# First and last units of a fused attention and FFN kernel replanned: identity first, beta's product in fp32r parts, last FFN pair in two jobs

## The reference, cut to what matters

```python
# x: (2, 1024, 256), 16 heads of 128, FFN 256 -> 256 with ternary weights
def layer(x):
    n = layernorm(x)                                  # eps 1e-5, no gamma and beta
    q, k, v = (einsum('bsd,hed->bhse', n, W) for W in (W_Q, W_K, W_V))
    scores = where(causal, -1e9, einsum('bhse,bhme->bhsm', q, k) / sqrt(128))
    z = einsum('bhsm,bhme->bhse', softmax(scores), v)
    x = x + einsum('bhse,hde->bsd', z, W_O)
    m = layernorm(layernorm(x)) * gamma + beta        # the inner one without gamma, beta
    w = clip(round(W / (mean(abs(W)) + 1e-5)), -1, 1)
    return x + einsum('bsi,oi->bso', m, w) + bias
```

## Time and profile before

| | us |
|---|---|
| median of 3 runs | 816.5 |
| lowest and highest | 816.1, 816.52 |
| the profiled execution's own time | 813.95 |
| its span (first to last instruction) | 811.9 |
| PE busy | 801.7 (99%) |
| DVE busy | 666.5 (82%) |
| ACT busy | 557.1 (69%) |
| POOL busy | 547.4 (67%) |
| DMA queue of SP | 57.0% of the 16 engines' span |

### The profile page before, as it was taken

The page is one execution under the profiler, slowest core; times in us unless marked ns, Lnnn a source line. Parts: engine busy times, 40 slices in busy tenths (PEclk is TensorE's granted clock), DMA queues, the critical chain, the costliest instruction groups (busy, mean ns, idle before and its releaser), DMA issues.

```text
span 811.9 us, 14642 instructions
## 1 busy us (share of the span) xinstructions
PE 801.7 (99%) x4846; PEld 722.6 (89%) x4846; DVE 666.5 (82%) x1470; ACT 557.1 (69%) x1031; POOL 547.4 (67%) x280
## 2 busy tenths in 40 slices
PE   8999999999999999999999999999999999999998
PEld 7988998888999898899888899888889888899887
DVE  8988787888787878878878878788878788878988
ACT  6877667667666667666766766766766766766684
POOL 6188755696666856768557885568665686676486
PEclk9999999999999999999999999999999999999999
DMA  6366766456656565666655676546656655555603
GB/s 189 82 147 146 176 140 142 117 132 170 141 137 143 137 153 128 138 151 149 162 124 119 149 175 144 140 108 146 167 132 143 145 128 130 130 137 137 144 13 105
DMA packets 57226, 111.49 MB, mean 137 GB/s; under 512 B 16960, under 2 KB 21184, under 8 KB 57152
## 3 DMA queue, kind: packets, MB, share of 16 engines
q1 hardware_dynamic: 57152, 110.56, 57.0%
HBM read 10.88 MB, written 2.10 MB: 16 GB/s over the span
## 4 chain that ended last, share of the span: by engine, by line
PE 92%; DVE 3%; SPq 2%; DMA 1%; POOL 1%; issue 1%; ACT 0%; POOLq 0%; ACTq 0%
PE scores L701 23%; PE ring L654 23%; PE ring L634 21%; PE ring L643 11%; PE ring L664 10%; SPq L452 2%; PE ring L673 1%; DMA pT<-turn 1%; PE ring L598 1%; PE scores L763 1%; POOL norm L544 1%; DVE acc L878 1%; DVE stats L896 0%; PE scores L691 0%; DVE scores L858 0%
## 5 line engine op out<-in xcount | busy, mean ns | idle before, releaser
L528 POOL TENSOR_TENSOR pT<-pT 128x1024 fp32r<-128x1024 f32 x186 | 444.7, 2412 | 251.7 <-ACT pT L799 251.6
L792 ACT ACTIVATE turn<-scores,negmax 128x128 f32<-128x128 f32 (+7 forms) x256 | 189.0, 739 | 154.5 <-DVE negmax L858 88.3
L858 DVE CUSTOM_DVE_ANT_0 scores<-scores,mask 128x128 f32<-128x128 f32 (+7 forms) x256 | 192.7, 763 | 101.7 <-PE scores L701 100.5
L701 PE MATMUL scores<-kT,qT 128*128 128x512 f32 (+2 forms) x1056 | 224.9, 350 | 1.2 <-ACT turn L792 1.2
L654 PEld LDWEIGHTS ring<-pT,v 128*128 128x128 f32 x1116 | 188.0, 189 | 24.8
L654 PE MATMUL ring<-pT,v 128*128 128x512 f32 x1116 | 209.8, 342 | 0.0
L799 ACT ACTIVATE pT<-pT 128x1024 fp32r<-128x1024 f32 x186 | 196.4, 1057 | 16.3 <-DMA pT<-turn 15.4
L701 PEld LDWEIGHTS scores<-kT,qT 128*128 128x128 f32 x1056 | 175.5, 188 | 20.6 <-ACT turn L792 2.2
L866 DVE STREAM_TRANSPOSE turn<-turn 128x128 f32<-128x128 f32 (+1 forms) x248 | 187.1, 764 | 0.0
L664 PE MATMUL ring<-wo_s,zT 128*128 128x256 f32 x768 | 113.3, 284 | 0.2 <-DVE zT L929 0.2
L878 DVE SCALAR_TENSOR_TENSOR acc<-ring,inv,acc 128x256 f32<-128x256 f32 x256 | 109.5, 469 | 0.0
(11 more groups left out here) (84 smaller groups left out, 553.4 us busy)
## 6 DMA issues: line engine op xcount, KB each, us to landing
pT<-turn SPq DMA_DIRECT2D x496, 128.0 KB, 2.3
pT<-turn SPq DMA_DIRECT2D x496, 64.0 KB, 2.0
acc<-in_x SPq DMA_DIRECT2D x8, 256.0 KB, 5.3
wk_raw<-in_wk SPq DMA_DIRECT2D x8, 256.0 KB, 2.9
wq_raw<-in_wq SPq DMA_DIRECT2D x8, 256.0 KB, 3.8
wv_raw<-in_wv SPq DMA_DIRECT2D x8, 256.0 KB, 3.0
norm<-in_wo SPq DMA_DIRECT2D x8, 256.0 KB, 2.9
out<-acc SPq DMA_DIRECT2D x8, 256.0 KB, 2.2
```

The source lines that it names most:

```text
L528: pool.tensor_tensor(chunk(half, LO, c), f32(chunk(half, LO, c)), f32(chunk(half, HI, c)), ALU.subtract).then_inc(plo_ready, 1)
L701: mm = pe.matmul(scores[:, t % 2, first + c:first + c + n], qT[:, par, a, t * P:(t + 1) * P], kT[:, par, m, c:c + n], start=(i == 0), stop ...
L792: act.activation(turned, columns, ACT.Exp, bias=negmax[:, t % 2:t % 2 + 1], scale=-1.0, accum_out=rowsum[:, u % 2, t:t + 1]).then_inc(prob ...
L858: dve.tensor_tensor_reduce(out=tile, in0=tile, in1=mask[:, S - (t + 1) * P:S], scale=-1.0, scalar=FAR, op0=ALU.add, op1=ALU.min, accum_out ...
```

## The change

The lists of the steady units stay as they are. The START and END lists are written anew with the same jobs, with these differences of content:

- POOL makes the identity and its copy before anything else, under a semaphore of their own (`ident_ready`), and PE waits for that alone. The mask follows. The clear of `turn1` moves from before the three weight splits to behind them.
- 50 instead of 48 warm-up products ahead, 30 instead of 34 behind the first two transposes.
- ACT's second `std` stands before its half of `("x", 1)` instead of behind it.
- POOL splits beta into two fp32r parts (`("beta",)`), and makes the ternary weights before its first norm instead of behind its third. The product with beta is four fp32r matmuls instead of two fp32 ones, and stands much earlier in the list.
- The last FFN pair is two jobs, `("ff", 7, 0)` and `("ff", 7, 1)`, each with an addition and a store of its own.

`tiles_of` and the new branch in `wait_norm` make room for a norm shared by two engines; no item in the lists uses it.

```diff
-WARM_UP = 48
+WARM_UP = 50
 START_TENSOR = (
-    ("x", 0), ("x", 1), ("warm", 34), ("qk", 2, 0), ("x", 2), ("x", 3), ("qk", 0, 0), ("qk", 0, 1), ("qk", 3, 0),
+    ("x", 0), ("x", 1), ("warm", 30), ("qk", 2, 0), ("x", 2), ("qk", 0, 0), ("x", 3), ("qk", 0, 1), ("s", 0, 0),
...
 START_SCALAR = (
-    ("std", 0), ("std", 1), ("norm", 0), ("norm", 1), ("x", 0), ("x", 1), ("std", 2), ("norm", 2), ("norm", 3),
+    ("std", 0), ("std", 1), ("norm", 0), ("norm", 1), ("x", 0), ("std", 2), ("x", 1), ("norm", 2), ("norm", 3),
...
@@ def store
-                sp.wait_ge(job_taken, job["ff", c] + 1)
-                tiles = slice(2 * c, 2 * c + 2)
+                sp.wait_ge(job_taken, job[("ff",) + item[1:]] + 1)
+                c, own = item[1], own_tiles(item)
+                tiles = slice(2 * c + own[0], 2 * c + own[-1] + 1)
@@ GpSimd
-            pool.memset(zero, 0.0).then_inc(const_ready, 1)
-            pool.memset(ident[:, :], 0.0).then_inc(const_ready, 1)
-            pool.memset(mask[:, :], 0.0).then_inc(const_ready, 1)
-            own = mask[:, S - P:S]
-            pool.wait_ge(const_ready, 3)
+            pool.memset(ident[:, :], 0.0).then_inc(ident_ready, 1)
+            pool.wait_ge(ident_ready, 1)
             pool.affine_select(out=ident[:, :], in_=ident[:, :], compare_op=ALU.not_equal, fill=1.0, base=0,
+                               pattern=[[-1, P]], channel_multiplier=1).then_inc(ident_ready, 1)
+            pool.wait_ge(ident_ready, 2)
+            pool.tensor_copy(ident_b[:, :], ident[:, :]).then_inc(ident_ready, 1)
+            def split_beta():
+                pool.wait_ge(small_in, 48)
+                pool.tensor_copy(beta_r[:, HI, :], beta_s[:, :]).then_inc(beta_ready, 1)
+                pool.wait_ge(beta_ready, 1)
+                pool.tensor_tensor(beta_r[:, LO, :], beta_s[:, :], f32(beta_r[:, HI, :]), ALU.subtract).then_inc(beta_ready, 1)
@@ TensorE
-                    for kd in range(KD):
-                        mm = pe.matmul(dst[:, 0:D], beta_s[:, kd:kd + 1].broadcast_to([P, P]), f32(wf_s[:, kd, :]),
-                                       start=(kd == 0), stop=(kd == KD - 1))
+                    for i, (kd, a) in enumerate([(kd, a) for kd in range(KD) for a in (LO, HI)]):
+                        mm = pe.matmul(dst[:, 0:D], beta_r[:, a, kd:kd + 1].broadcast_to([P, P]), wf_s[:, kd, :],
+                                       start=(i == 0), stop=(i == 3))
```

More of the change, by code:

```diff
@@ L144 @@
     ("wave", 1, 2, 30), ("wave", 1, 3, 30), ("out", 0), ("out", 1), ("out", 2), ("out", 3), ("out", 4), ("out", 5),
-    ("out", 6), ("out", 7),
+    ("out", 6), ("out", 7, 0), ("out", 7, 1),
 )
@@ L199, in exists @@
             return u % KINDS == (2 if item[1] == "v" else 3) and u < LAST - 1
-        return kind != "load"
+        if kind in ("flip", "wave", "hip", "lop", "pv"):
+            return 0 <= u < LAST
+        return 0 <= u <= LAST and kind != "load"
     def run_of(start, table, end):
@@ L414, in last_turn, with tiles_of, own_tiles @@
             return flat[:, t % HALF * keys:t % HALF * keys + (t + 1) * P]
+        def tiles_of(item):
+            c = item[1]
+            if len(item) == 3:
+                return (2 * c + item[2],)
+            return tuple(2 * c + j for j in range(2) if item + (j,) not in vector_norm)
+        def own_tiles(item):
+            return (item[2],) if len(item) == 3 else (0, 1)
         def wait_norm(engine, item):
@@ L495, in _ @@
                 else:
-                    store(item[1])
-            sp.wait_ge(stored, 16 * (NT // 2))
+                    store(item)
+            sp.wait_ge(stored, 16 * sum(i[0] == "out" for i in sync_run))
         @block.gpsimd
         def _(pool):
+            pool.memset(ident[:, :], 0.0).then_inc(ident_ready, 1)
+            pool.wait_ge(ident_ready, 1)
+            pool.affine_select(out=ident[:, :], in_=ident[:, :], compare_op=ALU.not_equal, fill=1.0, base=0,
+                               pattern=[[-1, P]], channel_multiplier=1).then_inc(ident_ready, 1)
+            pool.wait_ge(ident_ready, 2)
+            pool.tensor_copy(ident_b[:, :], ident[:, :]).then_inc(ident_ready, 1)
+            own = mask[:, S - P:S]
             pool.memset(zero, 0.0).then_inc(const_ready, 1)
-            pool.memset(ident[:, :], 0.0).then_inc(const_ready, 1)
             pool.memset(mask[:, :], 0.0).then_inc(const_ready, 1)
-            own = mask[:, S - P:S]
-            pool.wait_ge(const_ready, 3)
-            pool.affine_select(out=ident[:, :], in_=ident[:, :], compare_op=ALU.not_equal, fill=1.0, base=0,
-                               pattern=[[-1, P]], channel_multiplier=1).then_inc(const_ready, 1)
+            pool.wait_ge(const_ready, 2)
             pool.affine_select(out=own, in_=own, compare_op=ALU.is_ge, fill=MASKED, base=0,
                                pattern=[[-1, P]], channel_multiplier=1).then_inc(const_ready, 1)
-            pool.wait_ge(const_ready, 4)
-            pool.tensor_copy(ident_b[:, :], ident[:, :]).then_inc(const_ready, 1)
             splits = [0]
@@ L585, in _ @@
                     normalise(item)
+                elif item[0] == "beta":
+                    split_beta()
                 elif item[0] == "tern":
@@ L666, in project_o, with project_ffn @@
                 return mm
-            def project_ffn(c, dst):
-                for j in range(2):
+            def project_ffn(c, own, dst):
+                for j in own:
                     tok = (2 * c + j) * P
@@ L673, in project_ffn @@
                         mm = pe.matmul(dst[:, j * D:(j + 1) * D], xT[:, a, kd, tok:tok + P], wf_s[:, kd, :],
-                                       start=(j == 0 and i == 0), stop=(i == 3), skip_group_check=True)
+                                       start=(j == own[0] and i == 0), stop=(i == 3), skip_group_check=True)
                 return mm
@@ L913, in normalise @@
             def normalise(item):
-                kind, c = item
+                kind, c = item[:2]
                 dve.wait_ge(ln_step, ln_no[rstd_of("rstd2" if kind == "norm2" else "rstd", c)])
                 wait_norm_place(dve, item)
-                for t in (2 * c, 2 * c + 1):
+                for t in tiles_of(item):
                     last = dve.tensor_scalar(norm[:, t % 4, :], acc[:, t, :], mv[:, t, 0:1], rstd[:, t:t + 1],
```

70 lines of the change are left out of this document (37 added, 33 removed), and 47 rows, old and new, of tables (END_SCALAR, END_TENSOR, END_VECTOR, START_TENSOR).

## The result

The changed kernel takes 817.75 us in the median of 22 runs (815.4 to 820.62), the kernel before 815.27 us (22 runs, 812.58 to 818.48; the three runs shown before the prediction were among its slower ones). The ratio is 1.0029, with a 95% interval of 1.0018 to 1.0039. So the change made the kernel slower, by about 2.4 us. The forecast was "the same", 0.4 us less than before.

A forecast was written before the change was run, and what follows sets the result against it. PE bounds the steady part, DVE the tail; the start gains only by starting sooner. Start -1.0 and tail +0.6 (-1.2 + 0.1 + 1.7) give -0.4: 816.5 - 0.4 = 816.1 us, the same; range 814.4 to 818.0.

The forecast's parts named there:

- The start, -1.2 and +0.2: Start: freed first shift and sooner splits gain 1.2 us, a PE stall or two loses 0.2; sum -1.0 us.
- the 6 in 10 of the forecast: Start: chance that DVE's first shift goes ahead of POOL's LO of wq_s and escapes its wait.
- the 0.2 that I allowed: Start: loss in us for a stall or two of PE as tile 3's transposition moves along.
- the chain of the first waves: Start, first waves to score tile 7 of unit 1: 0.1 us of slack; rival that it gets longer, chance 0.11.
- DVE's idle time in the tail, -1.2: Tail: the new DVE queue wins 1.2 of the 1.4 us of idle time.
- 0.1 us of loss for it and 0 for the store: Tail: last addition in two halves costs DVE 0.1 us more; smaller stores count 0.
- the second 0.5 inside an addition: Tail: DVE's second shift comes 0.5 us before the end of a POOL addition and waits for that.
- 0.2, 0.5, 0.7 and 0.5: Tail: waits in us of DVE's four shifts for POOL instructions, in order.
- the 795.4 and 794.6 that I had worked out: Tail: times in us of DVE's second shift and of the start of POOL's run of additions.
- +1.7: Tail: four shift waits, 1.9 us less 0.13 lost before, all on DVE's chain.
- My bound of 5.0 for all four: Tail: upper bound in us of the shift waits, 4 x 1.25, if each just fails.
- the case with the caught first shift: Rival in the start: first shift held again, with waits in the tail; 817.1 us, chance 0.27.

The follow-up runs named there:

- with the gaps: Changed kernel with each of POOL's bias additions waiting until the one before is done; ratio to the kernel before 0.9989.
- the start alone: Changed kernel with the END lists and beta's fp32 product of the kernel before; ratio to the kernel before 0.9991.
- the probes: Three kernels without the computation: runs of four POOL instructions, mostly two-tensor additions, one DVE shift issued into each; longest holds 1.24 to 1.28 us.
- second profile: Profile of the changed kernel run once more, unaltered; ratio to the kernel before 1.0034, second tail shift 2.96 us.
- the kernel whose additions wait: Changed kernel with POOL's second bias addition waiting until the tail's second shift is done; ratio to the kernel before 0.9977.
- the end alone: Changed kernel with the START lists, warm-up products and constants of the kernel before; ratio to the kernel before 1.0055.
- shift asked for later: Changed kernel with the tail's second reciprocal and shift behind the next pair's statistics in DVE's list; ratio to the kernel before 1.0035.

## Why the prediction was wrong

The measured 817.75 us lies inside the forecast range, 814.4 to 818.0, but by luck: the forecast stood on 816.5 us for the kernel before, whose median over 22 runs is 815.27. Against that the change moved the time by +2.4 us where -0.4 was forecast.

**The start, -1.2 and +0.2: nearly right.** PE's first warm-up product came at 1.87 (forecast 2.0), the shift was free, the first product moved by -1.08. It was free by a narrow margin, asked for 0.19 us ahead of POOL's LO, as the 6 in 10 of the forecast had it: in nine profiles with this start and a two-tensor shift in it, it was free in eight and held once (1.14 us, with the gaps). The stall was twice the 0.2 that I allowed: the chain of the first waves, which had 0.1 us of slack, moved by 0.63 only, and so did the end of the start: -0.64 instead of -1.0. With the start alone the kernel lost nothing.

**DVE's idle time in the tail, -1.2: right.** DVE's idle time there fell from 1.42 to 0.35 us, and its work by 0.15. Without what the shifts took beyond 0.16 us each, the tail is 28.63 - 3.88 = 24.75 us, and before 26.10 - 0.13 = 25.97. Beta's product fell from 1.08 to 0.73 us where nobody waits, and the last pair in two jobs is worth nothing, about as forecast (I had counted 0.1 us of loss for it and 0 for the store).

**The step that failed: "the second 0.5 inside an addition".** That a shift waits for POOL's addition was right; how long it can wait was wrong. The four shifts met what they were forecast to meet: 0, 2.77, 0.59 and 0.52 us beyond their 0.16, where I had 0.2, 0.5, 0.7 and 0.5. The moments were right as well: counted from the last reciprocal of the sums, which came 1.86 us later than before, the second shift and the start of the additions stand within some 0.1 us of the 795.4 and 794.6 that I had worked out. The sum is +3.75 us instead of +1.7. The mis-sized term is the second shift. I took a held shift to wait for the instruction that it met, and so had a bound of 1.25 us for each; it waited for the run of three that POOL had queued. My bound of 5.0 for all four held, but the only weight that I gave to waits over 2.8 us was 0.04, in the case with the caught first shift. That term makes up 2.3 of the 2.7 us between the forecast -0.4 and the +2.3 that the parts below add up to.

The Trainium skill, in SBUF — State Buffer, SBUF: two separate sides, says that the pair of ports is given for a whole instruction. In the probes it was so: a held shift ended 0.02 us behind its addition. In the kernel the wait went over the ends of two further instructions, and the measurement decides. It also lets any GpSimd instruction that reads SBUF stand against DVE's two inputs; the probe's one-tensor instructions did not hold the shift.

**The step that was missing: PE's clock.** A stall of 3 us on the chain of DVE let PE stand idle for 3 us, and in 23 of 29 executions its clock then fell. What it costs is 0.7 us by the medians above, which is within their noise, and 0.3 and 1.1 us by the two profiles. In the first profile of the changed kernel it didn't fall, so that trace alone would not have shown it. The sum below leaves it out.

The parts add up: -0.64 in the start, -1.2 + 3.75 in the tail, +0.4 behind DVE's last addition (3.08 us for 2.68), together +2.3 us, beside a measured 2.4 to 2.5. I had put that +0.4 at nothing. Its cause is open: with two last jobs the stretch is 2.79 to 3.10 us in nine profiles, with one it is 2.68 to 2.70 in three with the END lists of before and 2.90 with the new ones. The remaining 2.5 us between the two profiled executions lie in the steady units (679.2 for 676.7 us from the first score tile of unit 2 to that of unit 30) and vary with the execution: the changed kernel had 677.0 in its second profile.

**Open.** Why the run holds the shift to its end at 797 us and not at 800 us in the kernel whose additions wait, nor at 802.74 us in the kernel before, nor in any of the 139 two-tensor shifts that the probes issued beside additions. The instant, the forms of the instructions and ScalarE beside them are ruled out, as far as the probes copy the kernel. Two things weren't tried: PE's products and the DMAs, which the probes leave out, and which shift it is. All four long holds are of the shift of pair 5, and the shifts of pairs 6 and 7 were never held past the addition that they met. With gaps there was no long hold, in the one profile taken; that queued additions suffice for one is not shown.

## What to carry to other kernels

When a replanned order closes the idle time of one engine, look at what that idle time kept apart: here POOL's gap of 3.29 us had kept its additions away from the shifts at 797.32 and 797.93 us, the second by 0.04 us. Price a meeting of two engines on a shared resource by one instruction at least and by the whole run that is queued at most, give the upper price a real chance, and add what the engine downstream loses when it stands idle for that long. A tiny instruction on the critical engine is cheap to make immune (a per-partition scalar instead of a second tensor, at 0.17 us more for two columns), or the other engine is given gaps (0.14 us each) if it has time to spare. And with effects of 0.3%, time the same kernel in a second batch before believing a ratio.

## What the runs showed of the hardware

- A DVE instruction with two SBUF tensors waits for POOL's addition of two SBUF tensors: to its end in the probes (138 of 139 shifts, 0.15 to 1.28 us for an instruction of 0.15), and over three queued additions in three profiles of the kernel (2.92, 2.90, 2.96 us), over the last three of four in another (3.12). Elsewhere in the same kernels it waited for one (0.29 us in the kernel before, 1.06 with the second addition waiting).
- It does not wait for POOL's instructions with one SBUF tensor (0.144 to 0.149 us at six of seven phases; the 0.355 at the other isn't explained), nor does a DVE instruction with one tensor and a per-partition scalar wait for additions (0.195 to 0.202 us).
- Back-to-back POOL additions overlap by 0.02 to 0.07 us in the records; a wait of each on the one before opened 0.14 us between them, and in the one profile with it that was enough (0.49 us for the shift that had taken 2.92).
- PE pauses for 3 us in both profiles of the changed kernel, and its mean granted clock was lowered in 23 of 29 executions of that kernel, not in the other 6. In the profiles with such a pause it was at half, 1.2 GHz, for 3.4 us (the end alone, and the changed kernel's second profile), for 6.8 us (shift asked for later), or not at all (its first profile). In the start its rise came between 4.8 and 8.9 us in the profiles of the kernels, and eight transposes took 1.04 or 1.45 us accordingly.
